# Softplus of a selective-scan layer: absolute value and relu read from PSUM, no SBUF copy of the biased step size

## The reference

```
dt = jnp.einsum('blr,ir->bil', ts, Wdt)
delta = jax.nn.softplus(dt + dt_bias[None, :, None])
def step(s, inp):
    u_t, d_t, B_t, C_t = inp
    dA = jnp.exp(d_t[..., None] * A)
    dBu = d_t[..., None] * B_t[:, None, :] * u_t[..., None]
    s = dA * s + dBu
    y = jnp.einsum('bin,bn->bi', s, C_t)
```

## Time and profile before

| | |
|---|---|
| median of 3 runs | 2893.6 us (2881.7 to 2895.21) |
| the profiled execution | 2891.33 us |
| its span | 2889.4 us |
| busy PE / DVE / POOL / ACT | 2412.0 / 2494.8 / 2261.2 / 1757.7 us |
| DMA queue, share of 16 engines | 62.4% |

### The profile page before, as it was taken

One profiled execution on the slowest core, in us unless ns is written; L12 is line 12 of the kernel. 1 busy time (PEld: TensorE's weight loads), 2 busy tenths in 40 slices (PEclk: granted clock), 3 DMA queues, 4 the chain that ended last, 5 costly groups with the idle time before them and its releaser, 6 DMA issues. The chain is left out here.

```text
span 2889.4 us, 38162 instructions
## 1 busy us (share of the span) xinstructions
PE 2412.0 (83%) x12266; PEld 1949.8 (67%) x12266; DVE 2494.8 (86%) x3131; ACT 1757.7 (61%) x2995; POOL 2261.2 (78%) x1371
## 2 busy tenths in 40 slices
PE   6668879788787998889988899889988896599968
PEld 5556667567566776677766777667766775377757
DVE  5559999799888999899989989798988988999973
ACT  5456568667466666576657666667656667465532
POOL 2237859988977989689996889779896899889852
PEclk9789889899888999899998999889999997599979
DMA  7644563674686367955777376964678478355544
GB/s 266 224 149 161 183 228 114 227 258 128 226 286 238 120 203 254 326 163 185 233 262 275 124 221 224 315 211 148 222 256 287 132 263 300 111 192 189 189 163 142
DMA packets 293951, 606.65 MB, mean 210 GB/s; under 512 B 23024, under 2 KB 23792, under 8 KB 293744
## 3 DMA queue, kind: packets, MB, share of 16 engines
q1 hardware_dynamic: 293744, 604.13, 62.4%
HBM read 451.47 MB, written 152.57 MB: 209 GB/s over the span
## 5 line engine op out<-in xcount | busy, mean ns | idle before, releaser
L1893 POOL TENSOR_TENSOR sbuf<-dus,bring 128x1024 f32<-128x1024 f32 x512 | 1222.0, 2403 | 236.2 <-PE pt L1369 128.5
L1520 ACT ACTIVATE pa<-dls,cst 128x512 f32<-128x512 f32 x1024 | 691.4, 688 | 424.2 <-DVE sbuf L1694 416.7
L1369 PE MATMUL pt<-ident,sbuf 128*128 128x128 f32 x4096 | 662.8, 299 | 227.1 <-DVE sbuf L1694 100.6
L1369 PEld LDWEIGHTS pt<-ident,sbuf 128*128 128x128 f32 x4096 | 517.1, 153 | 392.9 <-DVE sbuf L1694 142.3
L1288 PE MATMUL pm<-xT,wring 128*128 128x512 f32 x2816 | 707.8, 400 | 12.7 <-ACT pm L1420 5.5
L1694 DVE TENSOR_TENSOR_SCAN sbuf<-pa,sbuf 128x512 f32<-128x512 f32 x512 | 607.7, 1209 | 61.6 <-ACT pa L1520 52.9
L1694 DVE TENSOR_TENSOR_SCAN sbuf<-pa,carry,sbuf 128x512 f32<-128x512 f32 x512 | 634.5, 1266 | 26.4 <-ACT pa L1520 18.7
L1705 DVE SCALAR_TENSOR_TENSOR acc<-pt,cT,acc 128x512 f32<-128x512 f32 x768 | 547.5, 737 | 76.2 <-PE pt L1369 72.4
L1300 PE MATMUL pm<-wring,act 128*128 128x512 f32 x2176 | 577.8, 408 | 30.4 <-DVE hd L1622 10.3
L1288 PEld LDWEIGHTS pm<-xT,wring 128*128 128x128 f32 x2816 | 518.5, 190 | 115.8 <-issue 15.3
L1311 PE MATMUL pm<-xT,wring 128*128 128x512 f32 x1536 | 430.5, 432 | 79.5 <-DVE hd L1644 27.4
(11 more groups left out here) (130 smaller groups left out, 2266.6 us busy)
## 6 DMA issues: line engine op xcount, KB each, us to landing
wring<-wsp SPq DMA_DIRECT2D x408, 512.0 KB, 4.5
bring<-b_d SPq DMA_DIRECT2D x256, 256.0 KB, 3.9
xn_d<-tb SPq DMA_DIRECT2D x24, 1024.0 KB, 9.8
xnb<-xn_d SPq DMA_DIRECT2D x19, 1024.0 KB, 7.9
x_d<-tb SPq DMA_DIRECT2D x16, 1024.0 KB, 6.2
u_d<-hd SPq DMA_DIRECT2D x64, 256.0 KB, 4.9
sg_d<-hd SPq DMA_DIRECT2D x64, 256.0 KB, 4.4
tb<-x_d SPq DMA_DIRECT2D x16, 1024.0 KB, 7.1
```

Of the source, the lines that this page charges most:

```text
L1369: ins = e.matmul(pt[u.pt[tt]][:, k * P:(k + 1) * P], sbuf[:, u.s3, k, tt * P:(tt + 1) * P], ident[:, :], is_transpose=True, start=True, st ...
L1520: e.activation(pa[k % 2][:, :], dls[:, k, :], ACT.Exp, scale=col(C_A + (4 * u.ig + k) * N + u.n)).then_inc(S.a_exp, 1)
L1893: e.tensor_tensor(sbuf[:, u.s3, h * m:(h + 1) * m, :], dus[:, h * m:(h + 1) * m, :], bring[:, u.s2:u.s2 + 1, :].broadcast_to([P, m, TC]), ...
```

## The change

ACT reads each dt bank twice, once as |z| with the bias straight into `spe` and once as relu with the bias straight into `spx`. The bias copy and the 128 x 1024 passes for |z| and relu are gone. A bank is free after its relu. The |z| read waits for `spe`, the relu read for `spx`. In chunk 0 DVE's last sum is a plain addition, since `spx` holds the relu already.

```
-            m.before = self.get(u.x)
-            m.xin = self.up(S.a_dtx)
-            self.bank_free[m.bank] = (m.xin,)
+            m.x_before, m.e_before = self.get(u.x), self.get(u.e)
+            u.abs, u.relu = self.up(S.a_dtx), self.up(S.a_dtx)
+            self.bank_free[m.bank] = (u.relu,)
...
-                        q.wait_ge(u.pe, *u.before)
-                        e.activation(soft_row[u.x][:, u.k, :], pm[u.bank][:, :], ACT.Identity,
+                        q.wait_ge(u.pe, *u.e_before)
+                        e.activation(soft_row[u.e][:, u.k, :], pm[u.bank][:, :], ACT.Abs,
+                                     bias=col(C_DTB + u.i)).then_inc(S.a_dtx, 1)
+                        yield
+                        q.wait_ge(*u.x_before)
+                        e.activation(soft_row[u.x][:, u.k, :], pm[u.bank][:, :], ACT.Relu,
                                      bias=col(C_DTB + u.i)).then_inc(S.a_dtx, 1)
...
-                q.wait_ge(u.xin, *u.e_before)
-                e.activation(ee, x, ACT.Abs).then_inc(s.abs, 1)
-                yield
...
-                yield
-                e.activation(x, x, ACT.Relu).then_inc(s.relu, 1)
...
-                e.scalar_tensor_tensor(soft_buffers(u)[0], x, 0.0, ee, ALU.max, ALU.add).then_inc(s.d, 1)
+                e.tensor_tensor(soft_buffers(u)[0], x, ee, ALU.add).then_inc(s.d, 1)
```

More of the change, by code:

```diff
@@ L789, in soft_start @@
             m = self.add("m", Unit("dt", c))
-            m.i, m.k, m.x, m.tsT = i0 + k, k, u.x, self.tsT[c]
+            m.i, m.k, m.x, m.e, m.tsT = i0 + k, k, u.x, u.e, self.tsT[c]
             m.bank, m.bank_before = self.bank()
             m.pe = self.up(S.p_dt)
-            m.before = self.get(u.x)
-            m.xin = self.up(S.a_dtx)
-            self.bank_free[m.bank] = (m.xin,)
+            m.x_before, m.e_before = self.get(u.x), self.get(u.e)
+            u.abs, u.relu = self.up(S.a_dtx), self.up(S.a_dtx)
+            self.bank_free[m.bank] = (u.relu,)
         if part == 3:
             self.free["tsT"] = (m.pe,)
-        u.xin = m.xin
-        u.e_before, u.w_before = self.get(u.e), self.get(u.w)
-        u.abs, u.exp, u.one = self.up(s.abs), self.up(s.exp), self.up(s.one)
+        u.w_before = self.get(u.w)
+        u.exp, u.one = self.up(s.exp), self.up(s.one)
         if c:
-            u.one2, u.q, u.relu = self.up(s.one2), self.up(s.q), self.up(s.relu)
+            u.one2, u.q = self.up(s.one2), self.up(s.q)
         else:
@@ L1203, in macaron @@
             s = Soft()
-            s.abs, s.exp, s.one, s.one2 = sem(f"s{name}_abs"), sem(f"s{name}_exp"), sem(f"s{name}_one"), sem(f"s{name}_one2")
-            s.q, s.relu, s.ln, s.l = sem(f"s{name}_q"), sem(f"s{name}_relu"), sem(f"s{name}_ln"), sem(f"s{name}_l")
+            s.exp, s.one, s.one2 = sem(f"s{name}_exp"), sem(f"s{name}_one"), sem(f"s{name}_one2")
+            s.q, s.ln, s.l = sem(f"s{name}_q"), sem(f"s{name}_ln"), sem(f"s{name}_l")
             s.d, s.du = sem(f"s{name}_d"), sem(f"s{name}_du")
@@ L1660, in dve_soft @@
                 yield
-                q.wait_ge(u.l)
+                q.wait_ge(u.l, u.relu)
                 if u.stay:
                     q.wait_ge(u.small)
-                e.scalar_tensor_tensor(soft_buffers(u)[0], x, 0.0, ee, ALU.max, ALU.add).then_inc(s.d, 1)
+                e.tensor_tensor(soft_buffers(u)[0], x, ee, ALU.add).then_inc(s.d, 1)
                 yield
```

## The result

| | before | after |
|---|---|---|
| median | 2893.6 us | 2918.12 us (2910.5 to 2923.63) |
| the profiled execution | 2891.33 us | 2923.63 us, span 2921.8 us |
| ratio of the two kernels | | 1.0095 [1.0066, 1.0124] |

The account below looks back on a forecast made before the run. A ring of DVE, PE and POOL tied by in-order waits, DVE nearest to full, was taken as the bound. Terms -0.9 - 0.9 + 0.9 + 2.2 = +1.3 on 2891.3 gave 2892.6, stated as 2892 us; range 2870 to 2918 us.

Parts of the forecast that it names:

- ACT's work: On ACT, 128 bank reads at 0.684 us replace copies and passes: net -19.2 us, of which -0.9 us reaches the end.
- the first rival: Faster: the scan waits for ACT's exponential, so nearly all 19.2 us plus the opening return, 2871 us; faster had chance 0.25.
- The opening: Before POOL's first scan product, eight reads replace four copies and two passes: -0.9 us, on the path.
- DVE in chunk 0: DVE's last sum changes from max-and-add to add; both took 1.23 us undisturbed, so no effect.
- Banks: Each dt bank is freed about 0.57 us later; PE waits +1.7 us in three places, half counted, +0.9 us.
- the norm between the two reads: In post, the norm delays pm1 by 4.8 us; DVE late 1.5 us at three parts, half of 4.5 us counted: +2.2 us.
- The new interleaving: All engines' merged order shuffled only in the small, at most 28 of 1201 DVE rows: 14 us either way, centred on nothing.
- The second rival: Slower: in post, y blocks and projection groups delay PE's turning of states at three new places, 2918 us; slower had chance 0.27.
- its two signs: Signs of PE held in post: PE waits for L1437 above 5 us in total, or POOL waits for L1368 above 150 us.

Follow-up runs that it names:

- reads_together: Changed kernel with both reads of a bank planned and issued as one step, so nothing stands between them, planned anew; ratio 1.0133, 2933.31 us.
- old_instr_new_order: Instructions of the kernel before (copy, wide passes) issued in the order planned for the changed kernel; ratio 1.0152, 2938.61 us.
- before_part3_earlier: Kernel before with part 3 of a chunk's step sizes asked for at block 1 of ffn2 instead of block 4; ratio 1.0003, 2894.53 us.
- after_margin_020_parts23: Changed kernel with MARGIN 0.2 and step-size parts 2 and 3 asked for earlier, after blocks 1 and 6 of prep_in; ratio 0.9948, 2883.28 us.
- before_margin_031: Kernel before with the planner's MARGIN at 0.31 in place of 0.3, no instruction changed; ratio 1.0107, 2925.06 us.
- after_dwell_10: Changed kernel with the planner's DWELL at 10 instead of 12 us; ratio 1.0081, 2917.89 us.

## Why the prediction was wrong

**ACT's work: right.** 64 reads at 0.686 us and 64 at 0.689 us, where I took 0.684. With the order kept, ACT's busy time fell from 1757.7 to 1736.0 us, 21.7 us for the 19.2 of the sum. The Trainium skill, page "ScalarE: Activation LUTs", section "What ACT_TABLE_LOAD costs", gives 280 ns and 0.833 ns per element for an ACTIVATE with one column operand, an estimate of 0.707 us here; the rows of both reads are 0.02 us below that. How little of this counts was right too: the scan's wait for the exponential is 74.5 us, not shorter, and with the order kept ACT waited for the scan for 429.9 us instead of 416.7, 13 us more, where I had said 10 to 20. This is why the first rival, faster by 20 us, did not come.

**The opening: right in its own length, small beside what came before it.** From the first read to POOL's first product of the scan it was 17.5 us (177.23 to 194.73 us), against 18.46 us (175.34 to 193.8 us): 0.96 us shorter, where I had 0.9. But the first read began 1.9 us later, and the product came 0.9 us later than before. What delayed the first read I did not test.

**DVE in chunk 0: right.** The plain sum took 1.99 to 2.00 us per wide pass (L1662), and the max-and-add had taken 2.00 us (L1664), means over the four of each kernel.

**Banks, and the norm between the two reads: the mechanism is there, the norm's size was right and the rest too small.** PE waited 17.1 us in 10 places in the order of after, and in the old order 3.2 us against 0.8. Three of the 10 are the norm between two reads (in a fourth, 3.58 us, the norm stood ahead of both). The 22nd part, PE's last y block and DVE's use of it, in after:

```profile
1838.88 1.12 PE L1354 MATMUL pm<-ident,xT 128*128 128x128 f32 x4 [3.17 <-ACT spx L1437]
...
1840.03 0.76 DVE L1616 SCALAR_TENSOR_TENSOR pm<-act,cst,pm 128x512 f32<-128x512 f32 x1 [1.18 <-PE pm L1354]
```

At the three places PE waited 2.85, 3.17 and 3.68 us, and DVE behind it 0.73, 1.18 and 1.56 us, 3.5 us in all, where I had 4.5 us: this term was sized well. In the old order nothing stands between the reads, so of my terms only ACT, the opening and the banks apply, -0.9 us together. What all the new instructions cost there is 0.20 to 0.22%, some 6 us, so these terms are 7 us short and have the wrong sign. What the norm costs at the end was not tested; reads_together only shows that the loss is there without it.

**The new interleaving: the step that failed.** I wrote that the merge is "shuffled in the small; neither thread is run ahead of the other for long", and gave it an effect centred on nothing, of 14 us either way. The runs show that the new order costs 0.73% with the new instructions (1.0095 against 1.0022), 21 us, and 1.52% with the old ones (old_instr_new_order), 44 us, where the bound was 14 us. Three things were wrong in this step:

- *The sign.* An effect is centred on nothing if the order of before is an ordinary one. It isn't: both of its neighbours in MARGIN, the order of after and the three neighbours of that are 0.8 to 1.4% slower. Whether the constant was chosen by measuring I can't know; that it stands at a good place is measured.
- *The size.* I counted rows on DVE and took 28 of 1201 for small. On PE the same drift is up to 43 matmuls, on the average of an eighth, and it keeps one sign for five eighths. A drift of one sign is not averaged out as noise between stretches is; at the place in chunk 4 it ended in a load that wasn't there. It need not cost, though: before_part3_earlier has -45 and loses nothing. The bound by the deviation between stretches assumed that it is averaged out.
- *The wait.* The step sizes make a round trip through DRAM, and SP issues store and reload in a fixed order. I had not counted where that reload stands against the scan. In the seven stretches from 400 to 2500 us DVE's busy time fell from 1887.2 to 1863.5 us in all, so DVE was idle there for 23.7 us more, of the 32.3 us. The last of the seven, of after, against the earlier trace rows:

```profile
2200.00:2500.00 300.00, 241.75 (x1229) 194.34 (x1227) 250.64 (x312) 190.98 (x346) 247.74 (x143) 0.89 0.70 238
```

DVE is busy for 250.6 us of this stretch, where it was 260.0 us before; it contains POOL's wait of 11.92 us at 2397.75 us.

**The second rival** (PE held in post) gave the right time, 2918 us, for a reason that was at most a part, so the match is luck. Of its two signs one came, PE's waits for L1437 above 5 us (17.1 us), and the other didn't: POOL's wait for the turned states rose from 128.5 to 146.3 us, under the 150 I had set. The sign that came doesn't tell a good order from a bad one, since after_margin_020_parts23 has 13.8 us of it. Nor does the other: before_margin_031 has 129.7 us, as little as before, and after_dwell_10 111.3 us, less than before, and they are 1.1 and 0.8% slower.

**How far the cause is shown.** Shown: the order makes most of the loss, 0.73 of 0.95%, and in the old order the new instructions make the rest, 0.22%. What in the order costs the time is less sure. Shown is a relation: in all 20 kernels those with reload waits of up to 37.3 us are at 1.0023 or below, the one with 51.7 us is at 1.0030, and those with 55.7 us or more are at 1.0076 or above. Two pairs in which the only edit was the place of part 3, with a new plan each, moved both together (1.0030 to 0.9987, 1.0081 to 1.0017). Not settled: with the planner's own constants the same edit moved the wait from POOL to ACT and gained nothing (1.0091, 1.0087), and among the slow kernels the reload waits don't rank the times (62.9 us at 1.0141, 76.4 us at 1.0095). So a scan that runs ahead of the main work costs in more ways than by these waits, and I have no price for the others.

**A rival that I did not test** is TensorE's clock, which goes with the time as closely as the reload waits do. The mean granted clock over a kernel's runs was 0.901 to 0.910 in all kernels at 1.0076 or above, and 0.912 to 0.917 in those at 1.0030 or below; in both pairs above it rose (0.912 to 0.913, 0.908 to 0.913). The two levels are 1.2 and 2.4 GHz, and it was at the lower one all through 1830 to 1838 us of after, where PE was busy for 3.32 of the 8 us and which holds most of its wait of 3.17 us. So orders in which PE waits more may also get a slower PE, and no run separates the two. That the clock is not all of it one pair of executions shows: the profiled one of before_margin_031 took 2924.18 us and that of before 2891.33 us, both at 0.913, with PE busy for 2409.8 and 2412.0 us.

Open too is where the 8.4 us of the second read in the old order go, since PE's waits for it grew by 2.4 us only.

## What to carry to other kernels

Where a planner lays out all engines anew at each build, an edit is two changes: price the instructions in the old order by planning with the old ones, and treat the new order as one more draw; if the old order was better than its neighbours, the draw is more likely to lose than to gain. Before forecasting, run the old kernel with a constant of the planner moved a little, to see how ordinary its order is. Read the order of the queue that issues stores and reloads, and count how far one thread leads the other: a drift of one sign can end in a load that isn't there, and where a load that stood behind the store of the last part now stands ahead of it, look for a stall, as at the one place read here.

## What the hardware showed that I had not expected

A constant of the planner that changes no instruction moved the same kernel by 1.1% (before_margin_031), and across all orders of the same new instructions the time went from 2883.28 to 2935.35 us, 1.8%, at equal busy times on DVE, ACT and POOL within 7 us. Two reads of a PSUM bank, 0.69 us each, instead of one read and a wide pass later, cost about 8 us over 64 banks in the same order, although ACT's busy time differed by 3.5 us only.
